# Cross attention: the split of the row maxima moves to the front of GpSimd's phase, their transpose and negation move forward on TensorE and VectorE

## The reference

```
q = hidden @ Wq + bq;  k = context @ Wk + bk;  v = context @ Wv + bv
scores = einsum('bkgld,bksd->bkgls', q, k) / sqrt(8) + mask
attn = softmax(scores, axis=-1)
out = einsum('bkgls,bksd->bkgld', attn, v) -> (b, l, 256)
x = out @ Wo + bo + hidden
result = (x - mean(x)) * rsqrt(var(x) + 1e-6) * gamma + beta
```

## Time and profile before

| | us |
|---|---|
| median of 3 runs (lowest to highest) | 415.15 (414.96 to 417.97) |
| the profiled execution, its own time | 417.0 |
| span of the profile | 415.1 |
| PE busy | 321.5 (77%) |
| DVE busy | 265.5 (64%) |
| ACT busy | 220.7 (53%) |
| POOL busy | 214.6 (52%) |
| mean granted clock of TensorE | 0.935 of full |

### The profile page before, as it was taken

One profiled execution on the slowest core, in us unless ns is written; L12 is line 12 of the kernel. 1 busy time (PEld: TensorE's weight loads), 2 busy tenths in 40 slices (PEclk: granted clock), 3 DMA queues, 4 the chain that ended last, 5 costly groups with the idle time before them and its releaser, 6 DMA issues.

```text
span 415.1 us, 8012 instructions
## 1 busy us (share of the span) xinstructions
PE 321.5 (77%) x2560; PEld 200.5 (48%) x2560; DVE 265.5 (64%) x588; ACT 220.7 (53%) x498; POOL 214.6 (52%) x408
## 2 busy tenths in 40 slices
PE   4204171989998989999888888888888888888792
PEld 4203161655555666666555555555455555544321
DVE  7212350577776767777767777777677777777422
ACT  3100110666666666666666666666566666655550
POOL 2102430446665666666756566656466656553424
PEclk9999655899999999999999999999899999998967
DMA  7580593343333333333343333333333433340000
GB/s 233 152 252 3 163 343 104 96 111 95 93 93 101 98 102 102 99 102 105 88 112 92 93 95 98 96 105 106 113 97 108 111 106 108 110 115 22 15 15 25
DMA packets 35419, 44.40 MB, mean 107 GB/s; under 512 B 11824, under 2 KB 29488, under 8 KB 32816
## 3 DMA queue, kind: packets, MB, share of 16 engines
q1 hardware_dynamic: 35376, 43.86, 37.1%
HBM read 33.10 MB, written 9.96 MB: 104 GB/s over the span
## 4 chain that ended last, share of the span: by engine, by line
PE 34%; POOL 17%; DVE 15%; issue 15%; DMA 15%; SPq 4%; ACT 0%; POOLq 0%; DVEq 0%; ACTq 0%
PE oT_bank L619 9%; DMA q_stack<-max_parts 8%; PE t_bank L560 6%; PE s_bank L546 5%; DVE row_max L444 5%; PE misc_bank L646 4%; PE qk_bank L593 4%; DMA mask_sb<-mask 3%; POOL scaled L315 2%; POOL x_sb L319 2%; PE o_bank L634 2%; POOL rstd L310 2%; DVE attn L468 2%; DMA q_scratch<-q_parts 2%; SPq L244 2%
## 5 line engine op out<-in xcount | busy, mean ns | idle before, releaser
L444 DVE TENSOR_REDUCE row_max<-s_bank 128x4 f32<-128x512 f32 x256 | 172.1, 685 | 101.6 <-PE s_bank L546 101.4
L350 ACT ACTIVATE probs<-t_bank 128x512 f32<-128x512 f32 x256 | 149.5, 601 | 92.4 <-PE t_bank L560 91.7
L546 PE MATMUL s_bank<-k_stack,q_stack 72*128 72x128 bf16 x1024 | 103.0, 225 | 51.8 <-issue 24.1
L546 PEld LDWEIGHTS s_bank<-k_stack,q_stack 72*128 72x128 bf16 x1024 | 72.7, 100 | 123.1 <-DVE row_max L444 64.2
L560 PE MATMUL t_bank<-q_stack,k_stack 75*128 75x512 bf16 x256 | 99.5, 392 | 6.2 <-DMA q_stack<-max_parts 5.5
L619 PE MATMUL oT_bank<-probs,v_ones 128*32 128x512 f32 x512 | 71.7, 633 | 0.0
L359 ACT ACTIVATE qT<-qk_bank,bq_scaled 128x128 f32<-128x128 f32 x64 | 23.4, 365 | 59.7 <-issue 28.0
L315 POOL TENSOR_TENSOR scaled<-normed,rows_sb 128x256 f32<-128x256 f32 x32 | 23.2, 725 | 58.4 <-DVE normed L488 58.4
L593 PE MATMUL qk_bank<-act_sb,wq_sb 128*128 128x128 f32 x256 | 38.6, 300 | 5.3 <-DMA act_sb<-acts 4.4
L593 PEld LDWEIGHTS qk_bank<-act_sb,wq_sb 128*128 128x128 f32 x256 | 36.8, 213 | 5.9 <-issue 4.4
L308 POOL TENSOR_SCALAR var_eps<-mean_var 128x1 f32<-128x1 f32 x32 | 7.1, 223 | 61.2 <-DVE mean_var L483 61.2
(11 more groups left out here) (48 smaller groups left out, 355.5 us busy)
## 6 DMA issues: line engine op xcount, KB each, us to landing
q_stack<-q_scratch SPq DMA_DIRECT2D x32, 576.0 KB
q_scratch<-q_parts SPq DMA_DIRECT2D x32, 192.0 KB, 2.0
k_stack<-k_scratch SPq DMA_DIRECT2D x32, 144.0 KB
act_sb<-acts SPq DMA_DIRECT2D x1, 2048.0 KB, 10.4
result<-x_sb SPq DMA_DIRECT2D x16, 128.0 KB, 5.9
k_scratch<-k_parts SPq DMA_DIRECT2D x48, 32.0 KB, 1.9
x_sb<-x SPq DMA_DIRECT2D x1, 1536.0 KB, 14.2
act_sb<-acts SPq DMA_DIRECT2D x1, 1024.0 KB, 9.0
```

The source lines that it names most:

```text
L350: nc.scalar.activation(probs[:, u % 2, kv], t_bank[kv % 2][:], ACT.Exp).then_inc(exp_done, 1)
L444: nc.vector.tensor_reduce(row_max[:, u % 2, GROUP * kv:GROUP * (kv + 1)], s_bank[kv % 2][:].rearrange("p (g s) -> p g s", g=GROUP), AX.X, ...
L546: mm = nc.tensor.matmul(s_bank[kv % 2][:, g * S:(g + 1) * S], q_stack[0:TERM_ROWS, r, GROUP * kv + g], k_stack[0:TERM_ROWS, r, kv], start= ...
```

## The change

On POOL, `split_max(t - 1)` moves from the third place in the phase to the first, ahead of `add_bias`, `inverse_deviation` and `affine`. On PE, `transpose_max(t - 1)` moves from behind slot 2 to right behind slot 1, ahead of `probs_v(t - 3, 1)`. On DVE, `negate_max(t - 1)` moves from behind `maximum(t, 2)` and `standardise` to behind `maximum(t, 1)`, and `standardise(t - 4)` moves from behind `maximum(t, 2)` to behind `maximum(t, 3)`. No operation is added, dropped or resized. SP and ACT are unchanged.

```diff
--- before.py
+++ after.py
@@ -323,13 +323,13 @@
                 nc.gpsimd.partition_all_reduce(mask_any[:], mask_top[:], P, bass.bass_isa.ReduceOp.max).then_inc(flag_step, 1)
 
             def phase(t):
+                if live(t - 1):
+                    split_max(t - 1)
                 if live(t - 3):
                     add_bias(t - 3)
                 if live(t - 4):
                     inverse_deviation(t - 4)
                     affine(t - 4)
-                if live(t - 1):
-                    split_max(t - 1)
                 if live(t + 2):
                     split_q(t + 2)
                     if first_layer(t + 2):
@@ -508,13 +508,14 @@
                     moments(t - 4)
                 if now:
                     maximum(t, 1)
-                    maximum(t, 2)
-                if live(t - 4):
-                    standardise(t - 4)
                 if live(t - 1):
                     negate_max(t - 1)
                 if now:
+                    maximum(t, 2)
                     maximum(t, 3)
+                if live(t - 4):
+                    standardise(t - 4)
+                if now:
                     maximum(t, 4)
                 if live(t - 3):
                     normalise(t - 3)
@@ -667,11 +668,11 @@
                 if live(t + 2):
                     project_qk(t + 2)
                 slot(1)
+                if live(t - 1):
+                    transpose_max(t - 1)
                 if live(t - 3):
                     probs_v(t - 3, 1)
                 slot(2)
-                if live(t - 1):
-                    transpose_max(t - 1)
                 slot(3)
                 if live(t - 3):
                     transpose_o(t - 3)
```

## The result

The changed kernel takes 484.36 us (median of 4 runs, 482.29 to 485.77) against 415.64 of the kernel before (4 runs, 414.96 to 417.97): ratio 1.1638, interval 1.1581 to 1.1695. It is slower by 16%. The forecast was 467, the range 432 to 484. The profiled execution took 485.55 us, its span is 483.7; the mean granted clock of TensorE fell from 0.935 to 0.815.

What follows compares the result with a forecast made beforehand. PE's work was taken to bound one stretch of each phase, DVE's run to `attn` the other. The longer phases add 17.5 us, giving 433.6 as median; 33.6 for clock falls makes 467 us, range 432 to 484.

Steps and rivals of the forecast that it cites:

- The bound and the chain: GpSimd to DVE to PE: `rstd` queued behind the split that waits for DVE's negation, delaying `normed`, `attn` and L634.
- Steps 1 to 7: One phase timed from DVE's negations through GpSimd's queue to PE's transpose of `attn` (L634), reached at 260.22.
- stretch B: PE from slot 1's scores to the transpose of `attn` (L634): 5.35 us before, forecast 6.34, 0.99 longer.
- number 4: GpSimd: `add_bias`, taken to be like x_sb with a pitch of 0.68, puts `var_eps` at 257.54.
- The wait of `normed`: DVE: `normed` would wait about 1.2 us for GpSimd's `rstd` in each phase.
- DMA waits of `max_parts` vanish: `split_max` ends 3.3 us ahead of L634, so the DMA it feeds no longer holds up `t_bank` loads (10.2 us).
- Sum with the clock as it is: 27 phases take 299.2 us against 281.7, +17.5, without new falls of TensorE's clock.
- the faster rival: `standardise` does not wait because `rstd` ends before 257.2: 401 us, chance 0.03.
- its price is measured: TensorE's clock: each fall costs 1.4 us, 24 falls 33.6 us; only the number of falls called a judgement.
- The rival of longer lows: Low clock lasts through PE's next stretch, over 4 us a phase; in a quarter of phases 486 and more, chance 0.08.
- the weakest step: TensorE's clock falls in most phases because of PE's one longer gap: 24 times, bounds 18 to 28.
- Ramp and tail: Time outside the 27 phases: put at 0 within 1 us; phase 4 gains its own 0.99.

Runs made afterwards that it cites:

- Experiment 4: Changed kernel with GpSimd's order inverse_deviation, split_max, add_bias, affine: 409.62 us, ratio 0.9805 to the kernel before.
- Experiment 1: Changed kernel with GpSimd's order of before put back, TensorE and VectorE as changed: 428.99 us, ratio 1.0326 to the kernel before.
- Experiment 2: Changed kernel plus two unused matmuls of constants behind slot 5 in PE's gap: 438.60 us, ratio 1.0547 to the kernel before.
- Experiment 9: Changed kernel with GpSimd's order add_bias, inverse_deviation, split_max, affine: 400.43 us, ratio 0.9678 to the kernel before; with a filler matmul 401.98 us.
- 10: Changed kernel with GpSimd's order add_bias, inverse_deviation, split_max, affine, measured again in more rounds: 403.27 us, ratio 0.9648 to the kernel before.
- Experiment 5: Changed kernel with add_bias moved last on GpSimd, behind affine: 434.26 us, ratio 1.0441 to the kernel before.
- Experiment 3: Changed kernel plus one unused matmul of 256 columns behind slot 5 in each phase up to 32: 462.89 us, ratio 1.1086 to the kernel before.
- Experiment 11: Kernel before with only GpSimd's order changed, to add_bias, inverse_deviation, split_max, affine: median 450.66 us, four runs from 434.13 to 454.89.
- Experiment 6: Kernel before plus one unused matmul of 256 columns behind slot 5 in phases 14 to 32: 416.92 us, ratio 0.9975.
- Experiments 8: Changed kernel with GpSimd's order inverse_deviation, split_max, affine, add_bias, plus one 256-column filler matmul: 412.71 us, ratio 0.9875 to the kernel before.

## Why the prediction was right, point by point

**The bound and the chain: right.** The forecast said that `rstd` would be queued behind an instruction that waits for DVE, and that `normed`, maximum 4, the reciprocal, `attn` and L634 would follow it. Steps 1 to 7 gave 6.34 for stretch B; it measures 6.47. From slot 1's scores at 309.96 the split starts after 1.59 (1.60 forecast: 255.48 - 253.88), `x_bo` after 2.97 (2.98), `var_eps` after 3.77 (3.66), `rstd` ends after 4.64 (4.53), and L635 comes after 6.47 (6.34). By reported spans the prediction had 6.19, so the start-to-start spacing was the better ruler. The step that is off is number 4: the spacing from `x_bo` to `var_eps` is 0.80 and not the 0.68 read from `x_sb` to `max_rest`, +0.12. The spacing of the three splits (1.38) was exact.

**The wait of `normed`: 1.31 in a plain phase** for about 1.2 forecast. Experiment 4 shows that this wait makes the change slow: with `rstd` taken out from behind the split, and split_max still ahead of add_bias and `affine`, the wait and the slowdown vanish together. Experiment 1 removes the wait too and leaves 3% for another reason.

**DMA waits of `max_parts` vanish: right.** 0.7 us in 2 waits instead of 10.2 in 23.

**Sum with the clock as it is: 4.9 us short.** Experiment 2 measures it: its 27 phases take 405.23 - 101.17 = 304.1 us, the forecast was 299.2. Of this 27 x 0.13 = 3.5 are the step above; of the other 1.4, 16 phases of the first layer are 0.06 longer each, and one phase (22) is 0.4 longer than its like.

**The clock: right kind, nearly the right number, price too low.** I forecast 24 lows of 1.4 us, 33.6 in all. There are 21 lows, but 13 cost 1.6 and 8 cost 2.7: 346.2 - 304.1 = 42.1 us. (The prediction's sum for the faster rival has three falls within the 27 phases of before; the third, in phase 31, lies behind them.) The term that was mis-sized is "its price is measured": the price came from a low of before that began in the short gaps of that kernel, and the new gap gives a longer one. The rival of longer lows, 0.08, came true in 8 of 27 phases, near the quarter that it named, but at 2.7 us and not at the over 4 that it took; that the time lies nearer to its 486 than to 467 is in part chance. What I called the weakest step, the number, was the better one.

**Ramp and tail.** L635 of phase 4 lies 3.3 us later instead of 0.99, since the clock falls in phase 3 already (15.00 us from L635 to L635 instead of 11.71), and the tail is 0.8 longer; both were put at less.

These make up the difference in the profiled execution: 4.9 + 8.5 + 2.3 + 0.8 = 16.5 us between 469.1 (435.5 + 33.6) and 485.55. The time came out at the very end of the range, which had "up to 484 where a fall lasts on into the next stretch": two of the four runs are below 484, the median is 0.4 above it, and all lie outside the 458 to 478 of the bounds on the lows. So sign, mechanism and chain held; the size was off by 17 us, half of it from one low taken as typical, and the range reached that far by its width.

**The faster rival** put the point of decision at `rstd` before 257.2, with 401 us behind it if that held. Experiment 9 gets it there and measures 400.43 and, again, 403.27.

## What to carry to other kernels

Before an instruction that waits is moved ahead on an in-order engine, list what it overtakes, and when each result behind it is due: here `rstd` was due 1.3 us before the moved block could deliver it, and the right order was that in which the other engine makes the inputs. A wait of 1.3 us a phase cost about 36 us by itself (Experiment 2 against 9), of which the rest of the change gave 13 back, and 46 by TensorE's clock, so a change that lengthens PE's gap in a phase to between one and two microseconds has to be costed at the low clock as well, with more than one low as its price. A few matmuls on constants in the gap separate the two costs in a single run.

## What the runs showed of the hardware

- TensorE's clock against PE's idle time in a phase, all in this loop, one trace of each kernel: one gap of 0.59 or 0.73, no lows in the steady part (Experiments 1, 9 and 10); 0.74 to 0.89, none, and falls only where the gap had grown to 1.83 (Experiment 4); 0.44 and 0.70, two lows in the 27 phases and one in the phase behind them (before); 1.30 to 1.45, 5 of 27 (Experiment 5); 1.57 or 1.70, 12 of 27 (Experiment 3); 0.44, 0.71 and 0.5 to 0.6, 11 of the 16 phases that have all three (Experiment 11); 2.00 or 2.13, 21 of 27 (after). Waits of 0.58 and 0.98 near slot 0 were followed by one too (Experiment 6). The low is the level of 1.2 GHz (granted 0.50). The Trainium skill (TensorE: Matmul & The Clock Gate, A second HAM failure mode) describes short waits between groups of matmuls that make the clock go back and forth; the trace agrees, with 1.6 or 2.7 us a time.
- The longer lows come in a row. In phases 23 to 30 of the changed kernel each phase is as long as the next (13.56 to 13.65 us, eight times), while earlier ones with the same gap take 12.55 with phases of 10.94 in between; Experiment 11 has five in a row of 13.65 to 13.67. Why the kernel went from one pattern to the other isn't settled by any run here.
- DVE's tensor_scalar over 128x256 (`normed`) took 0.57 beside GpSimd's tensor_tensor `x_bo` (Experiment 4), and 0.40 or 0.41 in the plain phases of before, after and Experiments 8 and 9. The Trainium skill (SBUF — State Buffer, Who interferes with whom) says that this kind of operation can contend with GpSimd for a shared port pair, and that the loser waits until the other has finished. The trace agrees: `normed` ends 0.16 us behind the end of `x_bo`'s record whether it starts 0.31 behind `x_bo` and takes 0.57 (225.34 + 0.57 and 225.03 + 0.72) or starts 0.34 ahead of it and takes 1.21 (363.92 + 1.21 and 364.26 + 0.71).
